# First x and W1's group 0 loaded in quarters by turns, 16 matmuls on ones in place of 26, totals of the first maxima behind later products

## The reference, cut to what matters

```python
def _L0_cond_ref(x, indices, W1, b1, W2, b2, We, be):     # x: (16, 512, 512) f32
    h = gelu(einsum('bni,ih->bnh', x, W1) + b1, exact)     # W1: (512, 2048)
    shared_x = einsum('bnh,ho->bno', h, W2) + b2           # W2: (2048, 384)
    expert_x = einsum('bnh,bhp->bnp', h, We[indices]) + be[indices][:, None, :]   # We: (8, 2048, 128)
    return concatenate([shared_x, expert_x], axis=-1)
x = x + _L0_cond_ref(x, itok, W1, b1, W2, b2, We, be)
```

## Time and profile before

| what | value |
|---|---|
| median of 3 runs | 1221.32 us (1221.03, 1221.32, 1223.01) |
| the profiled execution's own time | 1223.01 us |
| its span in the profile | 1221.2 us |
| TensorE busy | 1205.5 us (99%) |
| VectorE busy | 1064.3 us (87%) |
| ScalarE busy | 767.8 us (63%) |

### The profile page before, as it was taken

How to read it: one execution, slowest core, us unless ns; L and a number is a source line. 1 busy time by engine, 2 the same in 40 slices (tenths; PEclk the granted TensorE clock), 3 DMA queues, 4 the chain that set the end, 5 groups by cost and what they waited for, 6 DMA issues and landing times.

```text
span 1221.2 us, 26275 instructions
## 1 busy us (share of the span) xinstructions
PE 1205.5 (99%) x10284; PEld 1008.6 (83%) x10284; DVE 1064.3 (87%) x1426; ACT 767.8 (63%) x1026; POOL 4.6 (0%) x12
## 2 busy tenths in 40 slices
PE   9998999999999999999999999999999999999998
PEld 4455657778888888888888888888888888888887
DVE  6986878788999889889988899888889888999886
ACT  3764546665766767666675666667567676667652
POOL 0000000000000000000000000000000000000000
PEclk9999999999999999999999999999999999999999
DMA  7334432012112121311212012121211213102101
GB/s 275 104 119 154 177 122 87 10 46 85 36 56 84 35 69 35 103 35 35 69 59 79 35 35 86 52 69 35 88 50 35 69 36 102 34 35 71 69 36 36
DMA packets 38833, 86.78 MB, mean 71 GB/s; under 512 B 5872, under 2 KB 6128, under 8 KB 36208
## 3 DMA queue, kind: packets, MB, share of 16 engines
q1 hardware_dynamic: 37616, 77.63, 18.8%
q0 software_dynamic: 1152, 8.39, 1.9%
HBM read 69.22 MB, written 16.78 MB: 70 GB/s over the span
## 4 chain that ended last, share of the span: by engine, by line
PE 83%; DVE 11%; issue 2%; DMA 1%; ACT 1%; DVEq 0%; SPq 0%; ACTq 0%
PE banks L1597 14%; PE banks L1599 13%; PE banks L1598 13%; PE q_ps L1597 8%; PE q_ps L1598 8%; PE q_ps L1599 8%; PE out_ps L1597 6%; PE out_ps L1599 6%; PE out_ps L1598 6%; DVE h_ring L936 2%; DVE x_lo L936 1%; DVE x_max L922 1%; DMA be_sb<-be_dram 1%; DVE w_max L922 1%; DVE w_lo L936 1%
## 5 line engine op out<-in xcount | busy, mean ns | idle before, releaser
L1597 PE MATMUL banks<-x_hi,w_hi 128*128 128x256 f16 (+1 forms) x1704 | 467.7, 274 | 3.9 <-ACT u L738 2.6
L1599 PE MATMUL banks<-x_hi,w_lo 128*128 128x256 f16 (+1 forms) x1704 | 467.9, 275 | 0.0
L1598 PE MATMUL banks<-x_lo,w_hi 128*128 128x256 f16 (+1 forms) x1704 | 467.8, 275 | 0.0
L936 DVE SCALAR_TENSOR_TENSOR h_ring<-u,scale,h_ring 128x1536 f16<-128x1536 f32 (+1 forms) x120 | 253.7, 2114 | 28.6 <-ACT h_ring L604 22.4
L716 ACT ACTIVATE kept<-banks 128x512 f32<-128x512 f32 x180 | 106.2, 590 | 179.7 <-PE banks L1599 179.6
L1597 PEld LDWEIGHTS banks<-x_hi,w_hi 128*128 128x128 f16 x1704 | 167.0, 98 | 34.3 <-ACT u L738 2.9
L1598 PEld LDWEIGHTS banks<-x_lo,w_hi 128*128 128x128 f16 x1704 | 166.9, 98 | 27.4 <-issue 0.5
L1599 PEld LDWEIGHTS banks<-x_hi,w_lo 128*128 128x128 f16 x1704 | 167.0, 98 | 22.0
L748 ACT ACTIVATE u<-u,b_sb,undo 128x512 f32<-128x512 f32 x120 | 91.2, 807 | 106.2 <-DVE u L1222 106.2
L1598 PE MATMUL q_ps<-h_ring,w_hi 128*128 128x256 f16 (+1 forms) x504 | 145.0, 288 | 0.0
L1597 PE MATMUL q_ps<-h_ring,w_hi 128*128 128x256 f16 (+1 forms) x504 | 145.0, 288 | 0.0
(11 more groups left out here) (181 smaller groups left out, 2081.0 us busy)
## 6 DMA issues: line engine op xcount, KB each, us to landing
out_dram<-x_raw SPq DMA_DIRECT2D x63, 256.0 KB, 2.4
x_raw<-x_dram SPq DMA_DIRECT2D x60, 256.0 KB, 4.0
t_sum<-w2o_dram SPq DMA_DIRECT2D x26, 512.0 KB, 3.8
t_sum<-we_dram SPq DMA_DIRECT2D x26, 512.0 KB, 4.3
w_sums<-we_dram POOLq DMA_DIRECT2D x8, 1024.0 KB, 5.1
h_ring<-w_dram SPq DMA_DIRECT2D x5, 1024.0 KB, 7.1
e_raw<-we_dram SPq DMA_DIRECT2D x3, 1024.0 KB, 4.9
t_sum<-w2p_dram SPq DMA_DIRECT2D x2, 1024.0 KB, 4.7
```

What stands on the lines that cost most here:

```text
L936: return nc.vector.scalar_tensor_tensor(to, of, s, hi, ALU.mult, ALU.subtract)
L1597: nc.tensor.matmul(ps, hi, v_hi, start=start, stop=False, skip_group_check=True)
L1598: nc.tensor.matmul(ps, hi, v_lo, start=False, stop=False, skip_group_check=True)
L1599: return nc.tensor.matmul(ps, lo, v_hi, start=False, stop=stop, skip_group_check=True)
```

## The change

Three edits. The loads of x and of W1's group 0 go out in quarters by turns, one chunk k each, with a semaphore for each quarter, and the waits of TensorE and VectorE follow the quarters. WARM goes from 26 to 16. The total of x's first maxima moves from behind (k = 0, c = 2) to behind (k = 1, c = 1), and that of W1's group 1 from behind (k = 2, c = 0) to behind (k = 3, c = 0).

```diff
-WARM = 26
+WARM = 16
...
-            half = 2 * BLOCK
-            for k in range(2):
-                sp.dma_start(x_raw[:, 0, KH * k:KH * (k + 1)], x[0, :, KH * k:KH * (k + 1)]
-                             ).then_inc(first_x_loaded[k], 16)
-                sp.dma_start(w1_raw(0)[:, half * k:half * (k + 1)], w1f[:, half * k:half * (k + 1)]
-                             ).then_inc(w1_rest_loaded if k else w1_loaded[0], 16)
+            for k in range(KC):
+                sp.dma_start(x_raw[:, 0, k], x[0, :, k]).then_inc(first_x_loaded[k], 16)
+                sp.dma_start(w1_raw(0)[:, BLOCK * k:BLOCK * (k + 1)], w1f[:, BLOCK * k:BLOCK * (k + 1)]
+                             ).then_inc(w1_rest_loaded[k - 1] if k else w1_loaded[0], 16)
...
             def first_x_top(k):
-                dve.wait_ge(first_x_loaded[k // KH], 16)
+                dve.wait_ge(first_x_loaded[k], 16)
...
                 if d == 0:
-                    dve.wait_ge(w1_rest_loaded, 16)
+                    for part in w1_rest_loaded:
+                        dve.wait_ge(part, 16)
...
                 for k in range(KC):
-                    if k % KH == 0:
-                        pe.wait_ge(first_x_loaded[k // KH], 16)
-                        pe.wait_ge(w1_loaded[0] if k == 0 else w1_rest_loaded, 16)
+                    pe.wait_ge(first_x_loaded[k], 16)
+                    pe.wait_ge(w1_loaded[0] if k == 0 else w1_rest_loaded[k - 1], 16)
...
-                        if k == 0 and c == 2:
+                        if k == 1 and c == 1:
                             pe.wait_ge(first_x_max_done, KC)
                             total(first_x_tops, first_x_max[:, :]).then_inc(first_x_all_done, 1)
-                        if k == KH and c == 0:
+                        if k == KC - 1 and c == 0:
                             w1_total(1)
```

More of the change, by code:

```diff
@@ L166, in build @@
         x_loaded = [sem("x_loaded_even"), sem("x_loaded_odd")]
-        first_x_loaded = [sem(f"first_x_loaded{k}") for k in range(2)]
+        first_x_loaded = [sem(f"first_x_loaded{k}") for k in range(KC)]
         w1_loaded = [sem(f"w1_loaded{d}") for d in range(D)]
-        w1_rest_loaded = sem("w1_rest_loaded")
+        w1_rest_loaded = [sem(f"w1_rest_loaded{k}") for k in range(1, KC)]
         w1_reloaded = sem("w1_reloaded")
```

## The result

| | before | after |
|---|---|---|
| median of 9 runs each, us | 1221.32 (1220.54 to 1224.31) | 1224.97 (1222.61 to 1226.08) |
| ratio after / before | | 1.0026, 95% interval 1.0016 to 1.0037 |
| profiled execution, its span, us | 1223.01, 1221.2 | 1224.02, 1222.2 |

The change made the kernel slower by 0.26%, about 3.2 us. I had forecast no change that could be told, 1221.8 in a range from 1220.0 to 1224.0; the median is above it.

What follows compares the result with a forecast made beforehand. It took VectorE's chain, started by x's total, to bound the start: 5.2 + 0.37 + 5.14 + 0.08 = 10.8 against 10.28, S = +0.5 us, so 1221.32 + 0.5 = 1221.8 us, range 1220.0 to 1224.0.

Steps and rivals of the forecast that it cites:

- VectorE's chain decides, and one number S counts: Start of kernel: VectorE sets the pace; S, the shift of x's total from 10.28, passes to the time; forecast +0.5 us.
- TensorE's start carries through: Rival: VectorE's chain has hidden slack, so TensorE's whole 2.1 us earlier start comes out, 1219.3 us; chance 0.10.
- F = 5.2: F is the time of TensorE's first f32 product, placed at 5.2 us with quarter loads; bounds 4.7 and 6.3.
- a slow start of the first quarters: Rival: the first quarters bear the slow loading, first product at 6.3, S = +1.2, 1222.5 us; chance 0.12.
- A first product after 6 us: Sign of being wrong, pointing to the loads: TensorE's first f32 product was expected at about 5.2 us.
- L = 0.37: Loss in us from early f32 products at half speed from 5.2 until the clock rises at 5.94.
- the clock rises late: Rival: a pause delays the clock's rise to 9.4 to 9.9, L about 2.2, 1223.7 to 1224.0 us; chance 0.12.
- x's data ready at 10.1, as before: x's last quarter lands at 9.4, one maximum follows; ready at 10.1 against 10.07 before, even for the total.
- Group 1's load costs 0: Issued at about 4.5 instead of 2.71, it lands no later and costs 0; +1 us kept for the range.
- The two pauses of TensorE behind the total: TensorE waits 1.7 us for group 1's lo, then about 1.1 us before the totals due at 27.31 + S.
- F + L + 5.22: Time of x's total behind six products: first product, clock loss, six products and the total; forecast 10.8 us.

Runs made afterwards that it cites:

- e5: The kernel before with only the two totals moved (half loads, 26 matmuls on ones): 1224.25 us, ratio 1.0029.
- e10: The kernel before without the four f32 products of chunk k = 1, group 1's total behind (k = 3, c = 1): ratio 1.0008.
- e11: The whole change plus matmuls on ones inside TensorE's two later long waits: 1222.32 us, 2.6 over the kernel before with the same fill.
- e13: The kernel before with quarter loads alone, plus matmuls on ones in the two later waits: 1222.21 us, 2.5 over before with that fill.
- e14: The kernel before with 16 matmuls on ones alone, plus the fill of the two later waits: 1222.03 us, 2.3 over before with that fill.
- e12: The change with WARM back at 26, plus matmuls on ones in the two later waits: 1221.90 us, 2.2 over before with that fill.
- e2: The changed kernel with both totals back in their old places: 1224.97 us, ratio 1.0034 to the kernel before.
- e1: The changed kernel with 26 matmuls on ones again: 1223.58 us, ratio 1.0023 to the kernel before.
- e3: The kernel before with 16 matmuls on ones and nothing else changed: 1223.02 us, ratio 1.0019.
- e7: The kernel before with each half load of x and W1 issued as two of 64 partitions; x's last piece late, no time or ratio given.
- e6: The kernel before with W1's group 0 cut after its first quarter and the loads reordered: 1222.46 us, ratio 1.0002.
- e8: The kernel before with four DMAs taking alternate chunks, packets of 2 KB; x's last piece as early as before, no time or ratio given.
- e4: The kernel before with the quarter loads alone (26 matmuls on ones, old totals): 1223.59 us, ratio 1.0023.

## Why the prediction was wrong, point by point

- *VectorE's chain decides, and one number S counts.* Right. A later total costs its delay (e5: +2.8 us and 1.0029, with nothing but the place of the totals), the lightened TensorE of e10 brought nothing, under the fill e11, e13 and e14 turn 2.2 to 3.0 us of shift into 2.3 to 2.6 us of time (e12 is off, 1.5 into 2.2), and the sixteen profiles add up. The rival in which TensorE's start carries through is refuted. One limit: after a lost clock TensorE can be the later one even at the last totals, by about 0.5 us in e2, e10 and e13.
- *F = 5.2.* Mis-sized: 6.25, the upper bound that I had named for a slow start of the first quarters. It was near 6.2 in e2 and e11 too. One us of S. A first product after 6 us was one of the signs of being wrong that I had named.
- *L = 0.37.* This is the step that failed most in the chain of the profiled execution: the rise at 5.94 of one trace was taken for that of the new program. It came at 10.65, and L was 13.66 - 6.25 - 5.22 = 2.2, the value of the rival "the clock rises late", to which I gave 0.12. The evidence against it that I quoted, a pause of 1.12 us that left the clock up, came after the rise; a pause before it was not covered. At the median this term is smaller: 16 against 26 matmuls is worth 0.4 us there (e11 and e12, and the change and e1), and the loss that is there with 26 too, 2.2 us under the fill, goes with the quarters and the moved totals. The Trainium skill ("TensorE: Matmul & The Clock Gate", "The two states you'll see"), which I had weighed, has the moment of the rise differ from run to run. The runs agree in kind: the same 16 matmuls had it up at 4.2 in e2 (they took 3.38 us, not 3.60) and left it down until 10.65 in the changed kernel, and it lay as late as 12.6 in e3. In size they do not: the page gives plus or minus 0.5 us for matmuls without a pause, and here 26 on end took 4.64 us in e7 and 5.73 in e12, which puts their rises about 2 us apart (an estimate: ten matmuls at 0.107 us in place of 0.213).
- *x's data ready at 10.1, as before.* This failed as well. In the changed kernel the last maximum ended at 10.93 + 0.69 = 11.6. So even with F = 5.2 and a full clock, S would have been +1.4, outside the forecast's own range. My error was to place landings by bytes ahead. The two windows under e6 speak against it, and the 252, 226 and 404 GB/s of the earlier trace rows can't be read as one load after the other. e8 clears the size of the packets. Whether the count of the loads, their size or the later issue of the last piece (3.66 in place of 1.66) makes the quarters late stays open.
- *Group 1's load costs 0.* Right. In the change it is covered, since VectorE comes for it at 16.71; with the quarters alone the cover is gone and it costs 0.6 us (e4).
- *The two pauses of TensorE behind the total*, 1.7 and 1.1 us: both measured as forecast, 1.70 and 1.07; they don't depend on S, so they came out right although S was wrong.
- *The sum.* F + L + 5.22 was the right formula, 6.25 + 2.2 + 5.22 = 13.7, S = +3.4 in place of +0.5. Of the 2.9 us by which S was mis-sized in the profile, F has 1.05 and L 1.8. Two rivals that I had counted one by one, the slow quarters (+1.2) and the late clock (+2.3), came together; for that the range had no room.

## What to carry to other kernels

A first look at which engine's chain sets the pace told truly that an earlier TensorE is worth nothing, but the same look says that whatever moves that chain's first event costs in full, so each of its conditions (data, place in the queue of another engine, clock) needs its own upper bound, and the bounds must be allowed to come together. In this kernel matmuls on ones are worth having up to the first real product (16 in place of 26 alone cost 2.3 us, e14), and long waits of TensorE are a place for them too: 44 of them took 1.6 us between the medians (ratio 0.9983) and most of the scatter out of a program of 1221 us. A kernel whose time scatters by 0.5% hides such differences; take the source of the scatter out first and then compare edits.

## What the runs showed of the hardware that I had not expected

- Eight DMAs for the first 2 MB had their last piece of x there 1.5 to 2.3 us later (10.25 to 11.08) than four (8.79 before). Four DMAs of 2 KB packets were as early (8.84) as four of 4 KB. The issue of the seventh load took 1.02 us in place of 0.43.
- Loads of 64 partitions moved 243 GB/s from 8.0 to 11.4 us with the DMA engines at a busy share of 1.07, loads of 128 partitions 410 at 1.02 before and 342 at 0.96 in the changed kernel (one profile each).
- After a wait the clock falls in some executions and not in others: at 0.50 from 98.1 behind a wait of 3.24 us before, at 1.00 behind one of 3.68 us in the changed kernel. A wait of 2.55 us was enough for it in e10, and one of 2.33 us in e7, while one of 2.31 us in e4 left it at 1.00.
- Two stretches of 3.4 us at the lower clock account for most of the scatter of this kernel: with the waits filled, the range went from 6.0 us (23 runs) to 1.3 (12 runs). The granted clock of each execution says the same: of the 23 runs of before, the six with a mean of 0.999 or more took 1218.93 to 1221.02 us, the twelve with 0.997 or less 1220.04 to 1224.94.
